# A graph network's sorting stage: bucket and target numbers read from PSUM by VectorE, totals in bank 7

## The chip, the cores and the metric

One core of one Trainium2 chip runs the whole program in one launch. The metric is the device time in microseconds (us) from the start of the execution to its end; the host only lays data out. The engines are TensorE (PE in the rows, PEld for its weight loads), VectorE (DVE), ScalarE (ACT), GpSimd (POOL) and SyncE (SP, which issues DMAs).

## The reference, cut to what matters

The graph has 6250 nodes with 128 features and 206250 edges, sorted by target node (`dst`); `src` is random. Four layers follow one another, each with a residual and a layer norm:

```python
edge_index = jnp.stack([src, dst])
x = _layernorm(x + _L0_gnn_ref(x, edge_attr_128, src, dst, ...))   # segment_sum of edge rows, 2-layer MLP
x = _layernorm(x + _L1_gnn_ref(x, edge_index, ...))                # attention over the edges
x = _layernorm(x + _L2_gnn_ref(x, edge_index, ...))                # edge MLP, segment_sum, node MLP
x = _layernorm(x + _L3_gnn_ref(x, edge_index, ...))                # normalised graph convolution
```

The change touches only the stage that computes the first layer's `segment_sum(edge_attr, receivers)` and, beside it, sorts the edges by source node for the three later layers.

## The kernel before, in words

Node features stay in SBUF, transposed, 128 features on the partitions. The edges are cut into 52 groups (`NG`) of 31 chunks (`G`) of 128 edges, 3968 edges a group, edge (p, c) of a group on partition p. The nodes fall into buckets of 128 for the sources, with one more for edges whose source is their target (`BUCKETS` is 50), and each group's targets lie in a window of 128 nodes.

The program is a row of blocks. "prepare" loads and splits the indices. Then comes "edge_sums_and_lists", the block of the change, which runs from about 107 to 812 us of the profiled execution. Each of its 52 steps does two things for one group.

The first is the sum of the edge rows by target. VectorE compares the numbers 0 to 127 with the 31 relative targets of each partition (`target_step`, L542) and so writes `dst_hot`, a float32 one-hot of 31 by 128. TensorE multiplies edge rows and one-hot, 31 products added up in PSUM bank 0 or 1 (`sum_step`, L609), and VectorE adds the result into the accumulator (`add_step`, L563). SyncE loads the edge rows, 2 MB a group, two groups ahead.

The second is the sort. VectorE compares the numbers 1 to 50 with the 31 bucket numbers of each partition (`buckets_dve`, L363) and writes `bucket_hot`, a bfloat16 one-hot of 31 by 50. TensorE counts each chunk's buckets (`totals_pe`, L369, into TOTALS in bank 2), ScalarE copies the counts to SBUF (L482), and TensorE forms running counts (`prefix_pe`, L376 and L380, in banks 3 to 6). VectorE picks each edge's own count (`pick_dve`, L387, one input in PSUM, one in SBUF), reduces it to a rank (`ranks_dve`, L401), and compares the rank with the numbers 0 to 127, each stored four times in a row (`rank_hot_dve`, L405, both inputs bfloat16 in SBUF). Meanwhile GpSimd multiplies the bucket one-hot with the edges' two values (`pay_with`, L412, two instructions a step, all operands in SBUF). TensorE multiplies rank one-hot and values (`codes_pe`, L393, into CODES in bank 7), ScalarE copies the lists (L486), TensorE transposes them (`turn_step`, L626, into TURNED in bank 7), and ScalarE copies them (L491, L495) and stores them (L497).

The order of work is written out by hand, one queue per engine, and semaphores join the queues:

- VectorE: pick and reduction of step j, bucket comparison of j+1, rank one-hot of j (it waits for the codes of j-1), target comparison of j+1, addition of j (it waits for the sum of j).
- TensorE: transposition of j-1, sum of j (it waits for the target one-hot of j), totals of j+1 (for the bucket one-hot), prefixes of j+1 (for ScalarE's copy of the totals), codes of j (for GpSimd's values, the rank one-hot and `turned_sb`).
- GpSimd: the values of j once the bucket one-hot of j is there and the codes of j-1 are done.
- ScalarE: values copied for GpSimd, the totals, the lists, the transposed lists.

`target_step` and the totals' part of TensorE's queue read so:

```python
def target_step(j, g, b):
    dve.wait_ge(summed0, j + 1)
    dve.tensor_tensor(dst_hot[b][:, :, :], over_chunks(iota, G), over_columns(of_group(rel, g), P),
                      ALU.is_equal).then_inc(hot0, 1)
...
def totals_step(j, b):
    pe.wait_ge(bucketed, j + 1)
    pe.wait_ge(totals_sb, j + 1)
    totals_pe(bucket_hot[b]).then_inc(totals_ps, 1)
```

`iota` is a 128 by 128 float32 tile in SBUF with 0 to 127 in each row, `iota1` the same plus one; `over_chunks` repeats a row for each of the 31 chunks and `over_columns` each number along a row. Re-sorts in the later stages call `buckets_dve` once each (L881 on) and use TOTALS too.

## Time and profile before

| what | value |
|---|---|
| median of 3 runs | 6396.56 us |
| lowest and highest run | 6394.72 and 6401.42 us |
| the profiled execution's own time | 6402.61 us |
| its span in the profile | 6400.8 us |
| busy over the span: TensorE, VectorE, ScalarE, GpSimd | 88%, 69%, 32%, 21% |
| mean granted TensorE clock, as a share of full speed | 0.949 |

Busy shares over the whole span mix stages with different limits, so the rows below are all of the one stage, most of it between 200 and 800 us, where every step looks like the next. In the rows, an instruction's duration runs from its start to its end as recorded; consecutive instructions of one engine overlap by some tens of ns, so the length of a chain is read from start to start. A float32 matrix product shows up as two records (62 for 31 products).

### The profile page before, as it was taken

What the parts mean: (1) busy time and instruction counts of PE and PEld (TensorE: products, weight loads), DVE (VectorE), ACT (ScalarE), POOL (GpSimd) and SP (SyncE); (2) the same over time, 40 slices, a digit from 0 to 9 for tenths busy, and PEclk for the clock granted to TensorE, in tenths of its full rate; (3) what the DMA queues carried; (4) which work ended last, traced back from release to release, by engine and by line L of the source; (5) the groups of instructions that cost most, each with busy time, mean ns of one, the idle gap of its engine ahead of it and who ended that gap; (6) DMA issues with size and microseconds to landing.
All of it is one profiled execution on the core that took longest, in us unless ns stands there. A gap on an engine that the chain in (4) does not pass through costs nothing. (4 is left out here: it accounts for less than half of the span.)

```text
span 6400.8 us, 164226 instructions
## 1 busy us (share of the span) xinstructions
PE 5654.8 (88%) x58310; PEld 4935.2 (77%) x58310; DVE 4415.6 (69%) x7547; ACT 2021.1 (32%) x4615; POOL 1361.4 (21%) x1304
## 2 busy tenths in 40 slices
PE   3999987999999999999977799989999898789987
PEld 2888876888888888888865599989899897456656
DVE  7999933777777777777764566656666564378874
ACT  0000033333333333343433222222222221366641
POOL 1444455333333333333324200000000000300000
PEclk9999999999999999999989899999999998899976
DMA  7444312222222222222211232323333221100000
GB/s 119 154 152 152 146 54 87 85 82 82 85 85 81 84 88 84 83 84 85 84 39 39 75 106 104 111 101 106 105 107 107 101 105 50 47 17 0 0 1 22
DMA packets 206497, 528.37 MB, mean 83 GB/s; under 512 B 33555, under 2 KB 85398, under 8 KB 199318
## 3 DMA queue, kind: packets, MB, share of 16 engines
q1 hardware_dynamic: 195936, 518.35, 23.8%
q8 instruction: 350, 5.73, 0.4%
q10 hardware_dynamic: 10179, 4.02, 0.3%
q14 instruction: 32, 0.26, 0.0%
HBM read 485.12 MB, written 37.19 MB: 82 GB/s over the span
## 5 line engine op out<-in xcount | busy, mean ns | idle before, releaser
L1275 PE MATMUL ps<-kv_table,stage 128*128 128x256 bf16 x7644 | 1262.6, 274 | 65.3 <-DVE stage L1131 27.3
L1247 POOL TENSOR_TENSOR message<-message 128x512 f32<-128x512 f32 (+1 forms) x676 | 725.1, 1073 | 1511.8 <-ACT message L1209 1511.8
L1663 PE MATMUL ps<-a_table,stage 128*128 128x128 bf16 x7644 | 865.7, 223 | 87.7 <-issue 56.4
L1666 PE MATMUL ps<-window,stage 128*128 128x128 bf16 x7800 | 883.5, 223 | 0.0
L1290 PE MATMUL ps<-message,slot_hot 128*128 128x136 f32 x5200 | 782.4, 293 | 112.2 <-POOL message L1247 92.9
L1565 DVE TENSOR_TENSOR slot_hot<-iota,slots 128x512 f32<-128x512 f32 (+1 forms) x676 | 454.1, 672 | 614.6 <-PE ps L1678 604.8
L1278 PE MATMUL ps<-window,stage 128*128 128x128 bf16 x7800 | 866.7, 220 | 0.0
L1290 PEld LDWEIGHTS ps<-message,slot_hot 128*128 128x128 f32 x5200 | 653.0, 191 | 201.7 <-POOL message L1247 165.6
L1138 DVE TENSOR_TENSOR slot_hot<-iota,slots 128x512 f32<-128x512 f32 (+1 forms) x676 | 452.3, 669 | 499.0 <-PE ps L1290 499.0
L1678 PE MATMUL ps<-edge,slot_hot 128*128 128x130 f32 x4992 | 731.6, 290 | 70.3 <-issue 70.3
L1616 ACT ACTIVATE edge<-ps 128x512 f32<-128x512 f32 x624 | 374.0, 599 | 1303.6 <-PE ps L1678 1266.6
L1275 PEld LDWEIGHTS ps<-kv_table,stage 128*128 128x128 bf16 x7644 | 673.1, 98 | 110.4 <-issue 55.7
L1278 PEld LDWEIGHTS ps<-window,stage 128*128 128x128 bf16 x7800 | 659.5, 99 | 62.4
L1678 PEld LDWEIGHTS ps<-edge,slot_hot 128*128 128x128 f32 x4992 | 638.9, 198 | 83.7 <-issue 83.7
L1200 ACT ACTIVATE q_kept<-ps 128x512 f32<-128x512 f32 (+1 forms) x676 | 392.7, 581 | 885.2 <-PE ps L1278 885.2
L1663 PEld LDWEIGHTS ps<-a_table,stage 128*128 128x128 bf16 x7644 | 577.0, 100 | 102.8 <-issue 92.4
L1666 PEld LDWEIGHTS ps<-window,stage 128*128 128x128 bf16 x7800 | 562.8, 100 | 0.0
L1989 PE MATMUL ps<-pairs,y_window 128*128 128x512 bf16 (+1 forms) x2028 | 532.0, 371 | 25.5 <-ACT pairs L1957 25.4
L1202 ACT ACTIVATE message<-ps 128x512 f32<-128x512 f32 (+1 forms) x676 | 392.8, 581 | 461.2 <-PE ps L1290 461.2
L1957 ACT ACTIVATE pairs<-ps 128x512 bf16<-128x512 f32 (+1 forms) x676 | 387.0, 573 | 254.6 <-PE ps L1981 207.1
L1148 DVE TENSOR_REDUCE score<-product 128x32 f32<-128x512 f32 (+1 forms) x676 | 450.0, 666 | 23.4
L1144 DVE TENSOR_TENSOR product<-ps,q_kept 128x512 f32<-128x512 f32 (+1 forms) x676 | 448.1, 663 | 5.6 <-ACT message L1202 5.6
(335 smaller groups left out, 7619.2 us busy)
## 6 DMA issues: line engine op xcount, KB each, us to landing
stage<-lists SPq DMA_DIRECT2D x312, 768.0 KB, 4.1
edges<-in_edge_attr SPq DMA_DIRECT2D x52, 1984.0 KB, 7.7
stage<-lists SPq DMA_DIRECT2D x104, 896.0 KB, 5.5
window<-qkv_rows SPq DMA_DIRECT2D x52, 288.0 KB, 4.8
qkv_rows<-kv_table SPq DMA_DIRECT2D x26, 384.0 KB, 2.5
window<-ab_rows SPq DMA_DIRECT2D x52, 192.0 KB, 4.4
qkv_rows<-q_parts SPq DMA_DIRECT2D x26, 192.0 KB, 2.0
ab_rows<-a_table SPq DMA_DIRECT2D x26, 192.0 KB, 2.0
```

The costliest lines, as they stand in the source:

```text
L1138: dve.tensor_tensor(slot_hot[n % 2][:, 0:nt, :], over_chunks(iota1[:, :], nt), over_columns(slots[:, ds(g, 1), 0, 4 * b:4 * b + nt] .rearr ...
L1144: dve.tensor_tensor(product[:, 0:nt, :], kv_ps[n % 2][:, 0:nt, 0:D], q_kept[n % 2][:, 0:nt, :], ALU.mult).then_inc(product1, 1)
L1148: dve.tensor_reduce(score[:, 0:nt, :].rearrange("p t h -> p (t h)"), product[:, 0:nt, :].rearrange("p t (h c) -> p (t h) c", c=HEAD), AX.X ...
L1247: pool.tensor_tensor(values, values, message[n % 2][:, 0:nt, D:D + HEADS].unsqueeze(3) .broadcast_to([P, nt, HEADS, HEAD]), ALU.mult).then ...
L1275: nc.tensor.matmul(kv_ps[n % 2][:, i, :], from_src, kv_table[:, tile, q, :], start=(q == 0), stop=(q == 2))
L1278: last = nc.tensor.matmul(q_ps[n % 2][:, i, :], own, window[d][:, q * D:(q + 1) * D], start=(q == 0), stop=(q == 2))
L1290: last = nc.tensor.matmul(ps[:, 6 + d, 0:D + HEADS], slot_hot[n % 2][:, i, :], message[n % 2][:, i, :], start=(tile == 0), stop=(tile == S ...
L1565: dve.tensor_tensor(slot_hot[n % 2][:, 0:nt, :], over_chunks(iota1[:, :], nt), over_columns(slots[:, ds(g, 1), 0, 4 * b:4 * b + nt] .rearr ...
L1663: nc.tensor.matmul(edge_ps[n % 2][:, i, :], from_src, a_table[:, tile, q, :], start=(q == 0), stop=False)
L1666: last = nc.tensor.matmul(edge_ps[n % 2][:, i, :], own, window[d][:, (3 + q) * D:(4 + q) * D], start=False, stop=(q == 2))
L1678: last = nc.tensor.matmul(ps[:, 6 + d, 0:D + EXTRA], slot_hot[n % 2][:, i, :], edge_of(d, b)[:, i, :], start=(tile == 0), stop=(tile == SELF))
L1989: last = nc.tensor.matmul(ps[:, 4 + quad % 2, 0:nt * P], y_window[:, ds(i * 4 + d, 1), q * D:(q + 1) * D] .rearrange("p s f -> p (s f)"), ...
```

## The change

The two rows of numbers are written once into PSUM bank 2 by TensorE (a product with the identity), on columns 128 to 383, and the two comparisons of the stage read them there. The totals, which had bank 2, go to bank 7, columns 256 on, beside CODES and TURNED; so the totals' product now also waits until ScalarE has copied the transposed lists of the step before (`turned_sb`). VectorE waits once for the numbers (`iota_set`). The re-sorts keep reading the SBUF row, and use the totals in bank 7. The one-hot of the ranks with its fours is not edited.

```diff
--- before.py
+++ after.py
@@ -351,16 +351,19 @@
         turned_sb = sem("turned_sb")
         lists_out = [sem(f"lists_out{b}") for b in range(2)]
         moved = sem("moved")
-        TOTALS = ps[0:G, 2, 0:BUCKETS]
+        iota_set = sem("iota_set")
+        IOTA_PS = ps[:, 2, P:2 * P]
+        IOTA1_PS = ps[:, 2, 2 * P:3 * P]
+        TOTALS = ps[0:G, 7, 2 * P:2 * P + BUCKETS]
         PREFIX = ps[:, 3:7, 0:8 * BUCKETS]
         CODES = ps[:, 7, 0:2 * BUCKETS]
         TURNED = ps[0:2 * TILES, 7, P:2 * P]
         GP = G + 1
         assert GP == 32 and 8 * BUCKETS <= 512 and 2 * TILES <= P
 
-        def buckets_dve(dve, hot, ids):
-
-            return dve.tensor_tensor(hot[:, 0:G, :], over_chunks(iota1[:, 0:BUCKETS], G), over_columns(ids, BUCKETS),
+        def buckets_dve(dve, hot, ids, numbers):
+
+            return dve.tensor_tensor(hot[:, 0:G, :], over_chunks(numbers[:, 0:BUCKETS], G), over_columns(ids, BUCKETS),
                                      ALU.is_equal)
 
         def totals_pe(hot):
@@ -531,15 +534,16 @@
                         dve.memset(bucket_hot[b][:, :, :], 0.0).then_inc(moved0, 1)
                         dve.memset(list_b[b][:, :, BUCKETS:TILES], 0.0).then_inc(moved0, 1)
                     dve.wait_ge(moved0, MOVE + 5)
+                    dve.wait_ge(iota_set, 1)
                     dve.sem_inc(moved, 1)
 
                     def bucket_step(j, g, b):
                         dve.wait_ge(paid, j)
-                        buckets_dve(dve, bucket_hot[b], of_group(bucket, g)).then_inc(bucketed, 1)
+                        buckets_dve(dve, bucket_hot[b], of_group(bucket, g), IOTA1_PS).then_inc(bucketed, 1)
 
                     def target_step(j, g, b):
                         dve.wait_ge(summed0, j + 1)
-                        dve.tensor_tensor(dst_hot[b][:, :, :], over_chunks(iota, G), over_columns(of_group(rel, g), P),
+                        dve.tensor_tensor(dst_hot[b][:, :, :], over_chunks(IOTA_PS, G), over_columns(of_group(rel, g), P),
                                           ALU.is_equal).then_inc(hot0, 1)
 
                     def rank_step(j, g, b, ahead):
@@ -564,7 +568,7 @@
 
                     with dve.Fori(0, total, PAIRS) as first:
                         dve.wait_ge(paid, first * 2 + 1)
-                        buckets_dve(dve, bucket_hot[0], of_group(bucket, 0)).then_inc(bucketed, 1)
+                        buckets_dve(dve, bucket_hot[0], of_group(bucket, 0), IOTA1_PS).then_inc(bucketed, 1)
                         target_step(first * 2, 0, 0)
                         rank_step(first * 2, 0, 0, True)
                         add_step(first * 2, 0, 0)
@@ -595,10 +599,13 @@
                     total = passes0(pe)
                     pe.sem_inc(prefixed, 1)
                     pe.sem_inc(coded, 1)
+                    nc.tensor.matmul(IOTA_PS, ident, iota, start=True, stop=True)
+                    nc.tensor.matmul(IOTA1_PS, ident, iota1[:, :], start=True, stop=True).then_inc(iota_set, 1)
 
                     def totals_step(j, b):
                         pe.wait_ge(bucketed, j + 1)
                         pe.wait_ge(totals_sb, j + 1)
+                        pe.wait_ge(turned_sb, j)
                         totals_pe(bucket_hot[b]).then_inc(totals_ps, 1)
 
                     def sum_step(j, pair, b):
@@ -627,6 +634,7 @@
                                          start=True, stop=True).then_inc(turned_ps, 1)
 
                     with pe.Fori(0, total, PAIRS) as first:
+                        pe.wait_ge(turned_sb, first * 2 + 1)
                         totals_step(first * 2, 0)
                         prefix_step(first * 2, 0)
                         sum_step(first * 2, first, 0)
@@ -880,7 +888,7 @@
                                          ALU.mult).then_inc(step, 1)
                 dve.tensor_scalar(r["dr1"], r["moved"], 1.0, None, ALU.add).then_inc(step, 1)
                 after(5)
-                buckets_dve(dve, r["hot"], r["bucket"]).then_inc(step, 1)
+                buckets_dve(dve, r["hot"], r["bucket"], iota1[:, :]).then_inc(step, 1)
                 after(9)
                 pick_dve(dve, r["chosen"], r["hot"]).then_inc(step, 1)
                 after(10)
```

## Rows read from the trace of the kernel before

**Rows 1.** Busy us (and instructions) of each engine, 200 to 800 us; then PEclk, DMA share, GB/s.

```profile
core 0: us, PE busy (x) PEld busy (x) DVE busy (x) ACT busy (x) POOL busy (x), PEclk, DMA share, GB/s
200.00:800.00 600.00, 545.74 (x7128) 484.73 (x7127) 593.00 (x269) 56.55 (x265) 276.07 (x90) 1.00 0.41 151
```

**Rows 2.** Groups by line, VectorE, 200 to 800 us.

```profile
line engine op names shapes xcount | busy us, mean ns | idle before us <-releasers
L542 DVE TENSOR_TENSOR dst_hot<-cst,rel 128x3968 f32<-128x3968 f32 x45 | 192.5, 4278 | 0.0
L363 DVE TENSOR_TENSOR bucket_hot<-iota,bucket 128x1550 bf16<-128x1550 f32 x45 | 143.0, 3178 | 0.0
```

**Rows 3.** Timeline, VectorE, one step: start us, duration us, instruction, idle time before.

```profile
400.14 1.81 DVE L387 TENSOR_TENSOR chosen<-ps,bucket_hot 128x1600 f32<-128x1600 f32 x1
402.10 1.82 DVE L401 TENSOR_REDUCE rank_all<-chosen 128x1600 f32 x1 [0.15 <-DVE chosen L387]
403.84 3.18 DVE L363 TENSOR_TENSOR bucket_hot<-iota,bucket 128x1550 bf16<-128x1550 f32 x1
406.94 2.28 DVE L405 TENSOR_TENSOR rank_hot<-rank_by,rank_all 128x4096 bf16<-128x4096 bf16 x1
409.14 4.28 DVE L542 TENSOR_TENSOR dst_hot<-cst,rel 128x3968 f32<-128x3968 f32 x1
413.35 0.27 DVE L563 TENSOR_TENSOR acc<-acc,ps 128x128 f32 x1
413.54 1.81 DVE L387 TENSOR_TENSOR chosen<-ps,bucket_hot 128x1600 f32<-128x1600 f32 x1
```

**Rows 4.** GpSimd's L412: two timeline entries, and its durations from 106 to 812 us.

```profile
131.94 7.04 POOL L412 TENSOR_TENSOR pay<-bucket_hot,vals 128x1550 bf16<-128x1550 bf16 x2 [10.59 <-PE ps L393]
...
399.19 6.20 POOL L412 TENSOR_TENSOR pay<-bucket_hot,vals 128x1550 bf16<-128x1550 bf16 x2 [7.20 <-PE ps L393]
...
L412 POOL TENSOR_TENSOR pay<-bucket_hot,vals x104: 2767/2954/6592, 112.0 to 804.8; 128x1550 bf16<-128x1550 bf16 x104
```

**Rows 5.** Timeline, TensorE, the same step: sum, totals, transposition, next sum.

```profile
400.07 7.19 PE L609 MATMUL ps<-dst_hot,edges 128*128 128x128 f32 x62 [0.55 <-DVE dst_hot L542]
407.19 0.97 PE L369 MATMUL ps<-bucket_hot,band 128*31 128x50 bf16 x31
...
412.65 0.26 PE L626 MATMUL ps<-ident_b,list_b 128*104 128x128 bf16 x1 [0.34 <-ACT list_b L486]
413.52 7.16 PE L609 MATMUL ps<-dst_hot,edges 128*128 128x128 f32 x62 [0.62 <-DVE dst_hot L542]
```

**Rows 6.** Timeline, TensorE: transpositions and sums, second, third and last step.

```profile
132.01 0.26 PE L626 MATMUL ps<-ident_b,list_b 128*104 128x128 bf16 x1 [0.34 <-ACT list_b L486]
132.30 7.16 PE L609 MATMUL ps<-dst_hot,edges 128*128 128x128 f32 x62
...
144.84 0.26 PE L626 MATMUL ps<-ident_b,list_b 128*104 128x128 bf16 x1 [0.34 <-ACT list_b L486]
145.43 7.16 PE L609 MATMUL ps<-dst_hot,edges 128*128 128x128 f32 x62 [0.33 <-DVE dst_hot L542]
...
802.23 7.19 PE L609 MATMUL ps<-dst_hot,edges 128*128 128x128 f32 x62 [0.56 <-DVE dst_hot L542]
```

**Rows 7.** Timeline, VectorE: block "prepare", and the first steps of the stage.

```profile
64.12 1.83 DVE L287 TENSOR_TENSOR rel<-rel,ps 128x1612 f32<-128x1612 f32 x1
...
109.19 0.06 DVE L532 MEMSET list_b<- 128x2 uint32 x1
110.01 1.77 DVE L363 TENSOR_TENSOR bucket_hot<-iota,bucket 128x1550 bf16<-128x1550 f32 x1 [0.76 <-DVE list_b L532]
111.70 4.29 DVE L542 TENSOR_TENSOR dst_hot<-cst,rel 128x3968 f32<-128x3968 f32 x1
...
136.27 4.86 DVE L405 TENSOR_TENSOR rank_hot<-rank_by,rank_all 128x4096 bf16<-128x4096 bf16 x1
```

**Rows 8.** Timeline, single instructions: ScalarE's copy, the last rank one-hot, a float32 product.

```profile
412.94 0.28 ACT L495 ACTIVATE list_i<-ps 104x128 int16<-104x128 f32 x1
...
806.00 3.70 DVE L405 TENSOR_TENSOR rank_hot<-rank_by,rank_all 128x4096 bf16<-128x4096 bf16 x1
...
819.46 0.58 PE L654 MATMUL ps<-cst,rank_max 128*1 128x128 f32 x2 [7.50 <-PEq L434]
```

## The prediction, made before the changed kernel was run

> **What bounds the kernel now.** The change touches one stage, the one named "edge_sums_and_lists", so I read that stage alone. First the table of busy time by stretch: from 200 to 800 us VectorE is busy 593.0 of 600 us, TensorE 545.7, GpSimd 276.1, ScalarE 56.6, and TensorE's granted clock is 1.00, its 2.4 GHz level [rows 1]. VectorE sets the pace, but TensorE is not far behind, and that distance caps what a faster VectorE can bring.
>
> Second, the groups by line on VectorE. The two comparisons that the change edits are L542 (targets, 3968 elements, 4278 ns) and L363 (buckets, 1550 elements, 3178 ns) [rows 2]. Per element that is 1.08 ns against 2.05 ns: the bucket comparison costs twice what its size asks for. In the stage's first step, with GpSimd not yet at work, the same line takes 1.77 us [rows 7]. So 1.41 us of each bucket comparison is not work.
>
> Third, the timelines of VectorE and GpSimd say what it is. The comparison starts at 403.84 and its result is there at 407.02 [rows 3]; GpSimd's two multiplications (L412) run from 399.19 to 405.39 [rows 4]. From 405.39 to 407.02 are 1.63 us, the 1550 elements at about 1.05 ns: it stood still until GpSimd was done, then ran. The pick (L387), whose first input is in PSUM, and the reduction (L401), with one input, lie under the same GpSimd work and take 1.81 and 1.82 us [rows 3]. Pick and target comparison differ by 2.47 us over 2368 elements, 1.04 ns each, which leaves 0.15 us fixed in either: not held. It works the other way too: the multiplications' fastest is 2767 ns, and the two together take 6.20 us instead of 5.54 [rows 4], since the first starts while the target comparison still runs.
>
> The Trainium skill (SBUF — State Buffer, section "Who interferes with whom") says that a VectorE instruction with two SBUF inputs and a GpSimd instruction that reads SBUF exclude each other for a whole instruction, and that one with at most one SBUF input does not contend. By that rule moving the numbers to PSUM ends the hold (my forecast); without it the rows leave a second reading, in which something else about the bucket comparison holds it, and the sum would be zero (the first rival). The trace agrees with the rule as far as it goes: held at L363, free at L387.
>
> **The change, part by part.**
>
> VectorE's step, from start to start: pick 1.96, reduction 1.74, bucket comparison 3.10, rank one-hot (L405) 2.20, target comparison 4.21, addition 0.19, sum 13.40 us [rows 3]. The sums on TensorE (L609) keep that pace: from 145.43 to 802.23 are 49 steps of 13.404 us [rows 6].
>
> *Bucket comparison, first input in PSUM.* Not held, it takes 1.69 us from start to start (110.01 to 111.70) [rows 7] instead of 3.10. VectorE's free step becomes 13.40 - 1.41 = 11.99 us. The price of a PSUM operand: the pick with one takes 1810 ns for 1600 elements; L287 with one, each number of it repeated, takes 1.83 us for 1612, the target comparison with both in SBUF 4.28 for 3968 [rows 3, 7]. Over 1.04 ns an element these leave 0.15, 0.15 and 0.15 us: within 0.01 us either way, and I take nothing.
>
> *Target comparison, first input in PSUM.* 4.28 us is its own length already (3968 at 1.04 and 0.15), so it stays. It only stops holding back GpSimd, whose pair shrinks from 6.20 to 5.54 us.
>
> *Rank one-hot.* It keeps two SBUF inputs. VectorE, now early, meets GpSimd with it. Reckon from the start of a sum: GpSimd starts 0.36 us before (131.94 against 132.30) [rows 4, 6] and ends at -0.36 + 5.54 = 5.18. The one-hot is held until then and needs 2.15 more (at 136.27 it shows 4.86 us and ends that much behind GpSimd's 138.98) [rows 4, 7]: 7.33. The next target comparison ends at 11.6, the addition and the pick follow, and the one-hot's next turn comes 11.99 after 5.18, at 17.17, or 4.3 into a step of 12.85: it waits 0.9 us, inside GpSimd's second multiplication. So VectorE has a hold left, in another place, and it is paid from slack: the targets are ready at 11.6, wanted at 12.85.
>
> *TensorE, the next bound.* A sum starts at 400.07 and the transposition (L626) at 412.65, 12.58 us; in between are the sum, totals, prefixes and codes without any wait for VectorE [rows 5]. What it waits for now is the target one-hot: from 412.65 to 413.52. Where the one-hot was nearly in time the sum came 0.29 us behind the transposition's start (132.01 to 132.30) [rows 6]. So its own step is 12.58 + 0.29 = 12.87; for the other parity 144.84 - 132.30 + 0.29 = 12.83. I take 12.85.
>
> *The new wait (totals for `turned_sb`).* Behind it on TensorE's queue stand totals, prefixes and codes. It asks for ScalarE's copy of the previous transposition (L495), which runs at 412.94 to 413.22 [rows 8]; the totals come 7.12 us after the sum's start (407.19) [rows 5], over 6 us later. The totals already stand behind two waits and start with no idle time. From below the price is nothing; a gain is excluded, since it removes nothing. From above it is 0.34 us, the idle time ahead of L626, where the awaited copy really comes last [rows 5], times 50 is 17 us. I take 0, the totals' own row being nearest.
>
> *Totals in bank 7.* Same 31 multiplications, same copy by ScalarE; ScalarE's other reads of that bank are 6 us away. Nothing.
>
> *Two matrix products for the numbers, and VectorE's wait for them.* Once only. TensorE has nothing to do until the first bucket comparison at 110.01 is done, and VectorE clears buffers until 109.25 and starts that comparison 0.76 us later [rows 7]. A product of this kind (float32, 128 columns) took 0.58 us [rows 8]; two are 1.2. They lie beside the clearing, which starts with the stage; with that cover gone they would cost 1.2 us once.
>
> *First and last step.* The second sum starts behind the first codes, and these behind the first sum, none of it behind VectorE [rows 6]: unchanged. At the end a held rank one-hot (806.00 to 809.70) is done 7.5 us behind the last sum's start at 802.23 [rows 6, 8]; by the reckoning above it is 7.3. Nothing.
>
> *Re-sorts in the later stages* keep their numbers in SBUF; the rest of the kernel is the same work, only sooner.
>
> **Sum.** From the second sum at 132.30 to the last at 802.23 are 669.93 us in 50 steps. At 12.85 they are 642.5. Saved: 27.4 us. VectorE's 1.41 a step would have been 71 us; 0.55 a step is what TensorE lets through. The profiled execution, 6402.6 us with a span of 6400.8, becomes 6375.2 with a span of 6373.4. It lies 6.0 us above the median of the runs, so against the 6396.6 us I say **6369 us**.
>
> **Rivals.**
>
> *The hold is not the port's* (chance 0.06). Some other trait of the bucket comparison, its bfloat16 output or second input, is slowed beside GpSimd. For it: in the steady steps it is the only slow instruction. Against: the pick has a bfloat16 second input too and is free, and the rank one-hot, where it met GpSimd, was held as well [rows 7]. VectorE stays at 13.40: 6397 us.
>
> *The hold moves instead of going* (0.04). The one-hot and GpSimd's second multiplication take turns, as at 131.94, where the pair took 7.04 us [rows 4]. Then the one-hot ends at -0.36 + 7.04 + 2.15 = 8.83, the targets at 13.1: a step of 13.1, 13 us saved, about 6384 us. Against: it needs VectorE to be there before the first multiplication is over, and a one-hot that follows the pick, which needs this step's prefixes, cannot be.
>
> *VectorE reads a broadcast row of PSUM slower while TensorE writes PSUM* (0.05), the slower side. At half rate the two comparisons' 5518 elements cost 1.04 ns more each, 5.7 us: 11.99 + 5.7 = 17.7 us a step, 4.3 more than now, over 50 steps 215 us: about 6612 us. It decides from 1.41/5518 = 0.26 ns an element upward, a quarter slower. For it: no row shows a PSUM row repeated over chunks. Against: the pick runs beside TensorE's sums at 1.04 ns.
>
> **How the numbers follow.** A measurement of this kernel can tell about 0.2%, 12.8 us. The forecast (0.85) and the rival of the moved hold just reach it. Faster 0.88, within 0.2% 0.07, slower 0.05. The low end of the range: 12.83 a step saves 28.4 us, and the runs lie 6.7 us apart: 6362. The high end: the new wait at its upper bound gives 6386, the moved hold 6384. What is left out is the first and the third rival, 0.11, and scatter.
>
> **What would show it.** Right: L363 at about 1.75 us in each step, the pick unchanged, L542 at 4.28; L412's pair at 5.5; L405 longer than 2.28, near 3.2, as the new holder of the wait; VectorE idle or held some 0.9 us a step; the sum no longer waiting for L542; sums 12.85 us apart and TensorE busy near 95% in the stage. Wrong: L363 still at 3.18 (first rival); L405 near 4.8 and L412's pair at 7 (second); L363 above 2.2 or L542 above 5.3 us with nothing on GpSimd (third); totals with idle time before them (the new wait).

## The result, and the profile after

The changed kernel took **6426.65 us** (median of 17 runs, 6404.69 to 6452.56), the kernel before 6396.56 us (17 runs on the same chip, 6383.01 to 6421.10). The ratio is 1.0042, 95% interval 1.0028 to 1.0056: slower by 0.4%, outside the 0.2% that a measurement can tell from nothing. The prediction, 6369 us (6362 to 6386) and 0.88 for faster, was wrong. The profiled execution took 6437.75 us with a span of 6435.9 us.

**The sort stage did what was predicted.** The table of busy time by stretch, changed kernel, the same columns as in [rows 1]; the last three rows are the edges of layer 1, the nodes of layer 1 and the edges of layer 2, which the prediction did not look at:

```profile
200.00:770.00 570.00, 540.91 (x7093) 481.52 (x7093) 563.16 (x267) 56.53 (x265) 244.19 (x89) 1.00 0.44 159
1047.80:3303.90 2256.10, 2083.41 (x20902) 1884.31 (x20902) 1665.85 (x3220) 869.49 (x2080) 725.42 (x676) 0.98 0.24 83
3303.90:3653.20 349.30, 241.47 (x1147) 173.18 (x1146) 157.78 (x407) 108.02 (x316) 110.84 (x208) 0.83 0.10 35
3653.20:5400.60 1747.40, 1612.54 (x20999) 1572.03 (x21000) 1091.94 (x1608) 402.65 (x727) 0.00 (x0) 0.93 0.30 105
```

In the first row TensorE is busy 540.9 of 570 us, 95%, against 91% in [rows 1]. VectorE seems as full as before (99%), but a part of that is now a held instruction. Its groups in the same stretch, and one step on its timeline (the counterparts of [rows 2] and [rows 3]; L546 is the target comparison, L366 the bucket comparison, L408 the rank one-hot, L390 the pick):

```profile
L546 DVE TENSOR_TENSOR dst_hot<-ps,rel 128x3968 f32<-128x3968 f32 x45 | 192.5, 4279 | 0.0
L408 DVE TENSOR_TENSOR rank_hot<-rank_by,rank_all 128x4096 bf16<-128x4096 bf16 x45 | 139.4, 3097 | 0.0
L366 DVE TENSOR_TENSOR bucket_hot<-ps,bucket 128x1550 bf16<-128x1550 f32 x45 | 79.3, 1762 | 0.0
```

```profile
401.85 1.82 DVE L404 TENSOR_REDUCE rank_all<-chosen 128x1600 f32 x1 [0.16 <-DVE chosen L390]
403.59 1.76 DVE L366 TENSOR_TENSOR bucket_hot<-ps,bucket 128x1550 bf16<-128x1550 f32 x1
405.27 3.21 DVE L408 TENSOR_TENSOR rank_hot<-rank_by,rank_all 128x4096 bf16<-128x4096 bf16 x1
408.40 4.28 DVE L546 TENSOR_TENSOR dst_hot<-ps,rel 128x3968 f32<-128x3968 f32 x1
```

The bucket comparison went from 3178 to 1762 ns, the target comparison stayed at 4279 against 4278 ns, and the one-hot, 2.28 us in [rows 3], is the new holder at a mean of 3.10: every step as forecast. GpSimd's pair and TensorE's step, the counterparts of [rows 4] and [rows 5]:

```profile
400.82 5.51 POOL L415 TENSOR_TENSOR pay<-bucket_hot,vals 128x1550 bf16<-128x1550 bf16 x2 [7.40 <-PE ps L396]
```

```profile
400.81 0.26 PE L633 MATMUL ps<-ident_b,list_b 128*104 128x128 bf16 x1 [0.34 <-ACT list_b L489]
401.03 7.16 PE L616 MATMUL ps<-dst_hot,edges 128*128 128x128 f32 x62
408.12 0.96 PE L372 MATMUL ps<-bucket_hot,band 128*31 128x50 bf16 x31
...
413.57 0.26 PE L633 MATMUL ps<-ident_b,list_b 128*104 128x128 bf16 x1 [0.34 <-ACT list_b L489]
413.87 0.35 PE L616 MATMUL ps<-dst_hot,edges 128*128 128x128 f32 x1
```

No idle time stands ahead of the sum (L616) any more, nor ahead of the totals (L372), behind the new wait. The second sum and the last:

```profile
132.34 7.16 PE L616 MATMUL ps<-dst_hot,edges 128*128 128x128 f32 x62
...
772.18 7.16 PE L616 MATMUL ps<-dst_hot,edges 128*128 128x128 f32 x62
```

These are 639.84 us in 50 steps, 12.80 each, against 13.40 in [rows 6]: 30.1 us saved, where 27.4 were forecast.

**The later stages gave it back, and more.** The first and last TensorE records of each stage divide both profiles (us; the sums by the start of their first and last record; the packets of code are explained below):

| kernel | sums | layer 0 begins | layer 0 | edges 1 | nodes 1 | edges 2 | nodes 2 | layer 3 | rest | packets of code: all, edges 1, edges 2 |
|---|---|---|---|---|---|---|---|---|---|---|
| before | 117.1 to 809.1 | 827.9 | 250.5 | 2224.6 | 332.9 | 1727.7 | 254.6 | 593.8 | 177.5 | 350, 101, 227 |
| changed | 117.0 to 779.1 | 797.8 | 250.0 | 2256.1 | 349.3 | 1747.9 | 254.7 | 593.7 | 177.2 | 476, 227, 227 |

The changed kernel enters layer 0 30.1 us sooner. Then it loses 31.5 us in the edges of layer 1, 16.4 in its nodes and 20.2 in the edges of layer 2, in code that the change does not touch. In which instructions, the groups on TensorE say (busy us, mean ns of one, idle time before them). The kernel before, edges of layer 1 (1078.4 to 3303 us), then of layer 2 (3635.9 to 5363.2):

```profile
L1275 PE MATMUL ps<-kv_table,stage 128*128 128x256 bf16 x7644 | 1262.6, 274 | 65.3 <-DVE stage L1131 27.3 <-issue 26.7 <-DVE product L1144 11.3
...
L1290 PE MATMUL ps<-message,slot_hot 128*128 128x136 f32 x5200 | 782.4, 293 | 112.2 <-POOL message L1247 92.9
...
L1666 PE MATMUL ps<-window,stage 128*128 128x128 bf16 x7800 | 883.5, 223 | 0.0
L1663 PE MATMUL ps<-a_table,stage 128*128 128x128 bf16 x7644 | 865.7, 223 | 87.7 <-issue 56.4 <-DVE stage L1546 31.3
L1678 PE MATMUL ps<-edge,slot_hot 128*128 128x130 f32 x4992 | 731.6, 290 | 70.3 <-issue 70.3
```

The changed kernel, the same two stages:

```profile
L1283 PE MATMUL ps<-kv_table,stage 128*128 128x256 bf16 x7644 | 1266.8, 275 | 97.8 <-DVE product L1152 60.8 <-DVE stage L1139 27.0 <-issue 10.0
...
L1298 PE MATMUL ps<-message,slot_hot 128*128 128x136 f32 x5200 | 786.2, 294 | 101.9 <-POOL message L1255 82.8
...
L1674 PE MATMUL ps<-window,stage 128*128 128x128 bf16 x7800 | 896.0, 225 | 78.1 <-issue 78.1
L1671 PE MATMUL ps<-a_table,stage 128*128 128x128 bf16 x7644 | 872.6, 225 | 88.0 <-issue 56.7 <-DVE stage L1554 31.3
L1686 PE MATMUL ps<-edge,slot_hot 128*128 128x130 f32 x4991 | 724.7, 289 | 0.0
```

In the edges of layer 1 TensorE stands idle 32.5 us longer ahead of one line, L1275, now L1283. Some 10 us of that come back ahead of L1298, which waits less for GpSimd than L1290 did, and 9.1 us are added because the same products take longer (busy 2083.41 against 2074.31 us): together nearly all of the 31.5. The timeline of L1283 there, changed kernel, only the entries with over 1.5 us of idle time before them, from the stage's start on:

```profile
1047.81 0.80 PE L1283 MATMUL ps<-kv_table,stage 128*128 128x256 bf16 x3 [27.00 <-DVE stage L1139]
1224.95 0.80 PE L1283 MATMUL ps<-kv_table,stage 128*128 128x256 bf16 x3 [2.92 <-DVE product L1152]
1312.01 0.49 PE L1283 MATMUL ps<-kv_table,stage 128*128 128x256 bf16 x3 [2.79 <-DVE product L1152]
1397.71 0.49 PE L1283 MATMUL ps<-kv_table,stage 128*128 128x256 bf16 x3 [2.98 <-DVE product L1152]
1485.42 0.80 PE L1283 MATMUL ps<-kv_table,stage 128*128 128x256 bf16 x3 [3.34 <-issue]
```

From 1224.95 on they are about 87 us apart, one for each turn of the stage's loop, and stand where the loop begins again. The cause that the row names is not to be trusted. VectorE's "product" (L1152) started at 1396.32 and took 0.68 us, so it was over at 1397.00, and the three records behind this idle time start at 1397.71; in other turns the same idle time is put down to "issue", that is, to nothing that the profile shows. In the kernel before such idle times stand at the head of some turns only: none between 1343 and 1516 us, where a turn began at about 1430. In the edges of layer 2 both kernels have two of them in every turn, which takes about 68 us: one at the loop's head (L1663, L1671), and one some 5 us later, once the code has run on a little. One turn of the kernel before, then one of the changed kernel:

```profile
3760.32 0.34 PE L1663 MATMUL ps<-a_table,stage 128*128 128x128 bf16 x3 [2.27 <-issue]
3765.75 1.46 PE L1678 MATMUL ps<-edge,slot_hot 128*128 128x130 f32 x6 [2.44 <-issue]
```

```profile
3777.83 0.43 PE L1671 MATMUL ps<-a_table,stage 128*128 128x128 bf16 x3 [2.49 <-issue]
3782.83 0.29 PE L1674 MATMUL ps<-window,stage 128*128 128x128 bf16 x1 [2.43 <-issue]
```

Counted from the loop's head, the second stands ahead of the 27th product before (24 gathering products, two of the eight at L1678, then the stop) and ahead of the 24th in the changed kernel: the same code stands still at another instruction.

What came with it is in the list of the DMA queues (packets, MB, share of 16 engines' time). The whole of the kernel before, and the whole of the changed one:

```profile
q8 instruction: 350, 5.73, 0.4%
```

```profile
q8 instruction: 476, 7.80, 0.5%
```

This queue brings code, in packets of 5.73 MB / 350 = 16.4 kB, taken here as 256 instructions of 64 bytes. Experiment 2 tests a shift by 256, and in experiments 3 to 6 the program of some 16,000 instructions on TensorE comes in 63 packets, about 256 to each. The change adds 126 packets, and the same list by stage puts all of them into the edges of layer 1: 101 before, 227 after. A stage without repeated fetching has 20 (see below), and 227 - 20 = 207 = 23 times 9: all 23 jumps back of the loop's 24 turns bring 9 packets. In the kernel before they were 101 - 20 = 81, 9 turns. The packets and the idle times go together turn by turn: in the kernel before, nine packets of code start between 1339 and 1414 us, around a turn that begins with idle time (at 1343), and none between 1416 and 1510 us, in the turn that begins without it.

**The theory** from this, ahead of the experiments: the two matrix products and the wait make TensorE's compiled program 9 instructions longer (8 of them the products, since a float32 product is two passes of a weight load and a multiplication) and shift all its later loops by 9 places. The other engines' programs have their old length. TensorE keeps its code in blocks of 256 instructions. The loop of layer 1's edges has 1702 instructions. Within 7 blocks it stays where it is; reaching into an eighth, it is fetched anew. Its head stands at place 100 of a block before and 109 after (places counted from 0), so that its last instruction has place 9 of an eighth block before, and 18 after (where the blocks begin was worked out from the places of the idle times, and is part of what is tested). The rivals: the kernel's later stages are slower by the 30 us by which they start sooner, or by a clock level that came by chance, or by PSUM's bank 2 or 7.

### The profile page after: what moved, and what is told of

The parts are those of the page before. It is cut to its first block and busy times, and to the rows that moved or that the text cites. A ratio compares the mean times of both kernels' runs of the same rounds, so it can differ in the third digit from the quotient of the medians.

```text
span 6435.9 us, 164235 instructions
## 1 busy us (share of the span) xinstructions
PE 5689.5 (88%) x58314; PEld 4961.9 (77%) x58314; DVE 4386.3 (68%) x7547; ACT 2021.6 (31%) x4615; POOL 1323.2 (21%) x1304
## 5 line engine op out<-in xcount | busy, mean ns | idle before, releaser
L1283 PE MATMUL ps<-kv_table,stage 128*128 128x256 bf16 x7644 | 1266.8, 275 | 97.8 <-DVE product L1152 60.8
L1674 PE MATMUL ps<-window,stage 128*128 128x128 bf16 x7800 | 896.0, 225 | 78.1 <-issue 78.1
L1671 PE MATMUL ps<-a_table,stage 128*128 128x128 bf16 x7644 | 872.6, 225 | 88.0 <-issue 56.7
L1298 PE MATMUL ps<-message,slot_hot 128*128 128x136 f32 x5200 | 786.2, 294 | 101.9 <-POOL message L1255 82.8
L1298 PEld LDWEIGHTS ps<-message,slot_hot 128*128 128x128 f32 x5200 | 657.0, 192 | 189.0 <-POOL message L1255 165.3
L1283 PEld LDWEIGHTS ps<-kv_table,stage 128*128 128x128 bf16 x7644 | 674.3, 99 | 146.0 <-DVE product L1152 71.6
L1671 PEld LDWEIGHTS ps<-a_table,stage 128*128 128x128 bf16 x7644 | 581.6, 101 | 103.0 <-issue 92.7
L1152 DVE TENSOR_TENSOR product<-ps,q_kept 128x512 f32<-128x512 f32 (+1 forms) x676 | 448.8, 664 | 5.7 <-ACT message L1210 5.7
```

The source lines that it names most:

```text
L1152: dve.tensor_tensor(product[:, 0:nt, :], kv_ps[n % 2][:, 0:nt, 0:D], q_kept[n % 2][:, 0:nt, :], ALU.mult).then_inc(product1, 1)
L1283: nc.tensor.matmul(kv_ps[n % 2][:, i, :], from_src, kv_table[:, tile, q, :], start=(q == 0), stop=(q == 2))
L1298: last = nc.tensor.matmul(ps[:, 6 + d, 0:D + HEADS], slot_hot[n % 2][:, i, :], message[n % 2][:, i, :], start=(tile == 0), stop=(tile == S ...
L1671: nc.tensor.matmul(edge_ps[n % 2][:, i, :], from_src, a_table[:, tile, q, :], start=(q == 0), stop=False)
L1674: last = nc.tensor.matmul(edge_ps[n % 2][:, i, :], own, window[d][:, (3 + q) * D:(4 + q) * D], start=False, stop=(q == 2))
```

## The experiments

Ten kernels, in three series, each with runs of the kernel before on the same chip (its medians: 6399.76, 6385.91 and 6401.00 us). Most add the same edit, fillers: increments of a semaphore that nobody waits for, in the block "prepare", ahead of all loops on TensorE. They do nothing but shift the code that follows.

```diff
                     last.then_inc(low_ready, 1)
+                    for _ in range(9):
+                        pe.sem_inc(pe_waited, 1)
```

**1. The kernel before, 9 fillers** (the shift without the change).

> The kernel before, with nothing but nine semaphore increments more on TensorE's queue, in the block "prepare", where TensorE waits for loads from 55 to 107 us. The changed kernel's TensorE program is nine instructions longer than before. Theory, placement: what costs the time is that the loops of the later stages lie nine instructions further on, so that the loop of layer1_edges (1702 instructions) has its code loaded anew on every turn: instruction queue 476 packets as after, against 350 before; layer1_edges about 2256 us against 2225; the kernel about 6440 us against 6397, slower although nothing of the sort is changed. Rival, the later stages suffer from the change's own edits (totals in bank 7, numbers in bank 2, another phase of the clock because the sort ends 30 us sooner): this kernel has none of them, 350 packets and 6397 us.

Measured: 6457.92 us (6446.75 to 6472.74), ratio 1.0103 [1.0064, 1.0141], 476 packets, 227 of them in the edges of layer 1, which took 2264.4 us. The slowdown comes without any of the change's parts, without an earlier start (layer 0 begins at 828.8) and without a new use of PSUM. The edges of layer 2 took 1747.9 us, exactly as in the changed kernel; the nodes of layer 1 took 336.8, near the 332.9 of the kernel before and not the 349.3 of the changed one. With the 31 us of experiment 4 taken off, 0.5%, this ratio would be 1.0055, within the interval of the change's own.

**2. The changed kernel, 247 fillers** (256 - 9, so that every loop has the place in its blocks that it had in the kernel before).

> The changed kernel with 247 semaphore increments at the same idle place, so that 9 + 247 = 256 instructions lie ahead of the later loops: by placement that is where they were before, if code is loaded in blocks of 256 instructions. Placement: about 350 packets plus one, give or take some turns (before, only some turns of layer1_edges loaded their code), layer1_edges near 2225 us, the sort's 30 us kept: about 6369 us. Rival, the change's own edits: 476 packets or so, later stages as after, about 6427 us.

Measured: 6367.34 us (6336.56 to 6388.06, 10 runs), ratio 0.9951 [0.9930, 0.9971], 324 packets, 74 in the edges of layer 1 (6 turns), 2203.7 us there. With the loops placed as in the kernel before, the change is 32 us faster (19 to 45 by the interval), where 27 were predicted. That the time lies 2 us from the predicted 6369 is partly luck: in its profile 6 turns fetched and not 9, which made the edges of layer 1 20.9 us shorter than in the kernel before. The edges of layer 2 took 1729.6 us (1727.7 before), and their second idle time is back ahead of the third of the eight products, as it must be if 256 places are a whole number of blocks:

```profile
3719.03 0.83 PE L1688 MATMUL ps<-edge,slot_hot 128*128 128x130 f32 x6 [1.61 <-issue]
```

**3 and 4. Both kernels, placed so that both loops fit within 7 blocks** (149 fillers in the changed kernel, 158 in the kernel before, which brings both to the same places).

> The changed kernel with 149 increments. By placement (loads of 256 instructions, eight kept at a time, the block boundary 64 instructions off as the stall at the window products of layer2_edges shows it: before the 27th matrix product after the loop's head in the changed kernel, before the 30th in the kernel before) both loops, 1702 and 1685 instructions, now lie in seven blocks each, and neither is loaded anew: about 350 - 91 - 217 = 40 packets; layer1_edges about 2190 us, layer2_edges about 1580 us (its 46 stalls of 2.2 to 4.0 us gone), the kernel about 6210 us. Rival: no effect, 6427 us; a partial one, if only one of the loops is freed: 227 packets fewer and 6370 us or 6250 us.

> The kernel before with 158 increments: the later loops stand where they stand in the changed kernel with 149. Placement: about 40 packets, layer1_edges and layer2_edges as long as in that kernel to within 5 us, and the kernel 27 to 30 us longer than it, about 6240 us: the change's own worth with placement held equal is -30 us. Rival, the change costs the later stages something of its own: this kernel would be faster than the changed one with 149.

Measured: 6136.15 us (6127.94 to 6142.63), ratio 0.9596 [0.9563, 0.9628], and 6167.17 us (6156.73 to 6180.07), ratio 0.9648 [0.9614, 0.9681]; 63 packets each. The times lie well under the expected 6210 and 6240 us, and 40 packets were expected: the direction was right, the size of what fetching costs was not. (The two products that the expectation names, the 27th and the 30th, are the 24th and the 27th in the traces.) The change is worth 6167.17 - 6136.15 = 31.0 us where the placement is the same. And the placement alone is worth 3.5% to the kernel before, far more than the change: 49.6 us in the edges of layer 1 and 198.3 in those of layer 2. Two other stages differ too, but in opposite directions and not by the placement: the nodes of layer 1 are 21.0 us longer, the "rest" is 19.8 shorter. Stage by stage:

| kernel | sums | layer 0 begins | layer 0 | edges 1 | nodes 1 | edges 2 | nodes 2 | layer 3 | rest | packets of code |
|---|---|---|---|---|---|---|---|---|---|---|
| changed, 149 | 118.4 to 780.6 | 799.4 | 250.6 | 2176.9 | 352.9 | 1529.4 | 254.7 | 593.3 | 157.7 | 63, 20, 19 |
| before, 158 | 117.9 to 809.4 | 828.4 | 251.2 | 2175.0 | 353.9 | 1529.4 | 254.7 | 593.4 | 157.7 | 63, 20, 19 |

The groups of experiment 3 on TensorE, first those of the edges of layer 1, then of layer 2:

```profile
L1285 PE MATMUL ps<-kv_table,stage 128*128 128x256 bf16 x7644 | 1252.9, 273 | 28.4 <-DVE stage L1141 27.6 <-DVE product L1154 0.8
...
L1676 PE MATMUL ps<-window,stage 128*128 128x128 bf16 x7800 | 861.3, 219 | 0.0
L1673 PE MATMUL ps<-a_table,stage 128*128 128x128 bf16 x7644 | 843.6, 219 | 31.3 <-DVE stage L1556 31.3
L1688 PE MATMUL ps<-edge,slot_hot 128*128 128x130 f32 x4985 | 696.3, 282 | 0.0
```

The 60.8 us put down to VectorE's product are 0.8, and every "issue" entry is gone; the one wait left is the stage's entry, the first turn's wait for the first gather one-hot. The table by stretch shows the edges of layer 2:

```profile
3579.50:5108.00 1528.50, 1528.25 (x20993) 1501.31 (x20994) 1091.31 (x1608) 402.22 (x726) 0.00 (x0) 1.00 0.34 117
```

TensorE is busy 1528.25 of 1528.50 us at a granted clock of 1.00, its 2.4 GHz level, where the changed kernel had 1612.54 of 1747.40 at 0.93. A fetch costs more than its idle time: of the 218 us between the two, 134.6 are idle time and 84.3 the same work done slower. The clock falls behind the idle times. The changed kernel ahead of a turn's two idle times (3775.3 to 3777.8 and 3780.4 to 3782.8), right behind them, and later in the turn:

```profile
3765.00:3775.00 10.00, 10.00 (x144) 9.94 (x142) 6.86 (x11) 2.79 (x5) 0.00 (x0) 1.00 0.21 80
3783.00:3787.00 4.00, 4.00 (x29) 3.91 (x29) 0.69 (x1) 0.60 (x1) 0.00 (x0) 0.50 0.01 4
3800.00:3840.00 40.00, 40.00 (x553) 39.41 (x550) 28.78 (x42) 10.52 (x19) 0.00 (x0) 1.00 0.37 127
```

The column behind the engines is the granted clock: 1.00, then 0.50 (its 1.2 GHz level), then 1.00 again.

**5. The bucket comparison's edit alone** (the target comparison reads SBUF again; products, waits and 149 fillers stay).

```diff
-    dve.tensor_tensor(dst_hot[b][:, :, :], over_chunks(IOTA_PS, G), ...
+    dve.tensor_tensor(dst_hot[b][:, :, :], over_chunks(iota, G), ...
```

> The changed kernel with 149 filler instructions (as the run before of that placement), whose target comparison reads its numbers from SBUF again, so that it costs about 0.05 us more or less; the bucket comparison keeps its numbers in PSUM. TensorE's code has the same length and place, so the code traffic should be the 63 packets of that run and the later stages its 1529 us in the edges of layer 2. Theory (the sort stage is bound by TensorE's 12.8 us per step once the bucket comparison is no longer held by GpSimd): sort stage within 1 us of the fully changed kernel (sums from 118.4 to 780.6), whole kernel within 10 us of 6136. Rival (the target comparison, 4.3 us long, takes a real part of the gain): steps of 12.9 us or more, the stage over 5 us longer, the whole at 6141 or more.

Measured: 6122.91 us (6111.77 to 6131.63), ratio 0.9597 [0.9562, 0.9631]. From the second sum to the start of the last record: 128.88 to 775.6, 646.7 us, as in experiment 3 (133.86 to 780.6, 646.7). The edit of the target comparison adds nothing to that of the bucket comparison; the rival is out. (The whole time is 13 us under the expected 6136; the kernel before was 14 us faster on this chip too, and the ratio is that of experiment 3.) The two groups, L368 the bucket and L548 the target comparison:

```profile
L548 DVE TENSOR_TENSOR dst_hot<-cst,rel 128x3968 f32<-128x3968 f32 x45 | 192.5, 4278 | 0.0
...
L368 DVE TENSOR_TENSOR bucket_hot<-ps,bucket 128x1550 bf16<-128x1550 f32 x44 | 77.5, 1762 | 0.0
```

**6. The target comparison's edit alone** (the bucket comparison reads `iota1` in SBUF again, at both calls).

```diff
-    buckets_dve(dve, bucket_hot[b], of_group(bucket, g), IOTA1_PS).then_inc(bucketed, 1)
+    buckets_dve(dve, bucket_hot[b], of_group(bucket, g), iota1[:, :]).then_inc(bucketed, 1)
```

> The changed kernel with 149 filler instructions, whose bucket comparison alone reads its numbers from SBUF again. Theory: it is held again until GpSimd's pair has ended, but the pair is shorter since the target comparison no longer slows it (5.5 instead of 6.2 us), so the chain of the step is worked out as 13.05 us against 13.40 before and 12.8 with both edits: the stage is some 12 us longer than with both, the whole near 6149. Rival A (the hold costs what it did before, the shorter pair brings nothing): steps of 13.4 us, the stage 30 us longer, the whole near 6167. Rival B (the hold was harmless): steps of 12.8 us, 6136.

Measured: 6132.36 us (6118.77 to 6150.33), ratio 0.9603 [0.9570, 0.9637], which the whole time does not set apart from experiment 5 (6149 us were expected, on the scale of the first series). The stage does: the sums run from 129.09 to 783.39, 50 steps of 13.09 us (13.05 expected, 13.40 and 12.80 the rivals). VectorE's groups, and its bucket comparisons and GpSimd's pairs in two steps:

```profile
L368 DVE TENSOR_TENSOR bucket_hot<-iota,bucket 128x1550 bf16<-128x1550 f32 x44 | 125.7, 2857 | 0.0
```

```profile
407.24 3.27 DVE L368 TENSOR_TENSOR bucket_hot<-iota,bucket 128x1550 bf16<-128x1550 f32 x1
...
420.73 2.46 DVE L368 TENSOR_TENSOR bucket_hot<-iota,bucket 128x1550 bf16<-128x1550 f32 x1
```

```profile
403.37 5.51 POOL L417 TENSOR_TENSOR pay<-bucket_hot,vals 128x1550 bf16<-128x1550 bf16 x2 [7.98 <-PE ps L398]
416.05 5.51 POOL L417 TENSOR_TENSOR pay<-bucket_hot,vals 128x1550 bf16<-128x1550 bf16 x2 [7.17 <-PE ps L398]
```

The pair is at 5.51 us although the bucket comparison waits on it. The second pair starts at 416.05 while the target comparison still runs (to 416.91), as in the kernel before, and is no longer slowed: it was the target comparison with two SBUF inputs that made the pair 6.20 us, as the prediction said. In experiment 5 it has two SBUF inputs again, and the pair still takes 5.51 us, because VectorE is early and the target comparison is over before the pair starts (409.22 against 410.04). The first comparison ends at 410.51, 1.63 us after its pair (408.88), the second at 423.19, 1.63 us after its pair (421.56): held again until GpSimd's end. The mean of the steps was right, but they are not even: the sums are 13.39 us apart here and 12.8 in the next step.

**7. The kernel before, 4 fillers** (the loop of layer 1 ends at place 13 of its eighth block).

> The kernel before with 4 filler instructions on TensorE ahead of all loops, nothing else changed. In the kernel before, the loop of the edges of layer 1 ends on the 9th instruction of its last block of 256 and its code was fetched anew on 9 of its turns; with 9 fillers it ends 9 instructions later and is fetched anew on every turn. Theory (a race between the fetch that runs ahead and the jump back, decided by how far into the last block the loop reaches): a number of turns between those two, so 350 to 476 packets of code, the edges of layer 1 at 2225 to 2256 us, the edges of layer 2 unchanged at 227 packets. Rival (another border passed between 0 and 9, or something that has nothing to do with the place): exactly 350 or 476 packets, by a jump.

Measured: 6395.28 us (6365.82 to 6412.91, 10 runs), ratio 1.0007 [0.9985, 1.0029]; 332 packets, 83 in the edges of layer 1 (7 turns), 2213.1 us there. Fewer than at place 9, not more, which fits neither side: the count did not grow with the distance, and two profiles with the loop at place 9 already differ by more (9 turns before, 6 in experiment 2).

**8. The kernel before, 246 fillers** (ten places back: the loop of layer 1 ends with the last instruction of its seventh block, that of layer 2 still reaches into an eighth).

> The kernel before with 246 fillers on TensorE ahead of all loops, so that by the block model the loop of the edges of layer 1 fits within 7 blocks of 256 instructions and ends with the last instruction of the seventh, while the loop of the edges of layer 2 still reaches into an eighth. Theory: the loop of layer 1 is fetched once (about 20 packets, 2176 us as in the runs without reloads), the loop of layer 2 is still fetched on every turn (227 packets, 1728 to 1748 us), about 270 packets in all, and the whole about 40 to 50 us under the kernel before. Rival (the fillers or the total length of the code matter, not where each loop lies): both loops change alike, either both near 20 packets (6167 us) or both above 200 (6450 us).

Measured: 6299.98 us (6290.45 to 6309.75), ratio 0.9869 [0.9834, 0.9905]; 270 packets, 19 and 227. The edges of layer 1 took 2176.2 us, as expected to the microsecond; those of layer 2 1691.1, under the 1728 to 1748 expected. The two loops are set apart by where each lies: the rival, fillers as such, is out. The whole is 86 us under the kernel before, where 40 to 50 were expected, in part because the fetches of layer 2 cost less here though as many packets came. Its second idle time stands at the same line (L1680 here is L1678 of the kernel before) but ahead of the last of the eight products, not the third: five products of two instructions, so the ten places. It is shorter in sum:

```profile
L1665 PE MATMUL ps<-a_table,stage 128*128 128x128 bf16 x7644 | 860.2, 222 | 84.7 <-issue 54.2 <-DVE stage L1548 30.5
L1680 PE MATMUL ps<-edge,slot_hot 128*128 128x130 f32 x4992 | 721.4, 287 | 52.0 <-issue 52.0
```

```profile
3726.59 0.27 PE L1680 MATMUL ps<-edge,slot_hot 128*128 128x130 f32 x1 [3.06 <-issue]
```

So with the same 227 packets the second idle time summed to 70.3 us in the kernel before, 78.1 in the changed one and 52.0 here.

**9. The change with one product instead of two** (the buckets' numbers 1 to 50 are columns 1 to 50 of the first product; real code in place of fillers).

```diff
-        IOTA1_PS = ps[:, 2, 2 * P:3 * P]
+        IOTA1_PS = ps[:, 2, P + 1:P + 1 + BUCKETS]
...
-                    nc.tensor.matmul(IOTA_PS, ident, iota, start=True, stop=True)
-                    nc.tensor.matmul(IOTA1_PS, ident, iota1[:, :], start=True, stop=True).then_inc(iota_set, 1)
+                    nc.tensor.matmul(IOTA_PS, ident, iota, start=True, stop=True).then_inc(iota_set, 1)
```

> The changed kernel with no filler, but with one product for the numbers instead of two: the buckets' numbers 1 to 50 are columns 1 to 50 of the first product's result. TensorE's code is 4 instructions shorter than the changed kernel's and 5 longer than that of the kernel before, so the loop of layer 1's edges reaches 14 instructions into its last block (9 in the kernel before, 13 with 4 fillers, 18 in the changed kernel). Theory (where the loops lie is all that the change lost by): the code of that loop is fetched anew on some turns only, 83 to 130 packets in it and 330 to 380 in all, the edges of layer 1 between 2205 and 2230 us, the sort stage as changed (sums to 779), and the whole near 6367, the time that was predicted for the change. Rival (14 is already too far into the block): 227 packets, 476 in all, 2256 us, the whole at 6425.

Measured: 6439.08 us (6422.74 to 6450.21, 6 runs), ratio 1.0057 [1.0035, 1.0079]; 476 packets, 227 in the edges of layer 1, 2264.4 us there. The rival was right: with its end at place 14, the loop is fetched on every turn. The forecast of a time near 6367 us for this kernel was wrong by 72 us.

**10. The kernel before, 7 fillers** (its end at place 16).

> The kernel before with 7 fillers, the loop of layer 1's edges ending 16 instructions into its last block. Theory (a race, more often lost the further the loop reaches in): between the 83 packets at 13 and the 227 at 18 in that loop, so some 90 to 200, 340 to 450 in all. Rival (a hard border between 13 and 18): exactly 227, 476 in all, or no more than the 83 to 101 seen at 13 and 9.

Measured: 6461.60 us (6443.71 to 6483.66), ratio 1.0079 [1.0049, 1.0109]; 476 packets, 227 in the edges of layer 1, 2266.3 us. The rival again. Together, by where in its eighth block the loop of layer 1's edges ends (one profile for each entry):

| place of the last instruction in the eighth block | packets there | turns with a fetch, of 23 | edges 1, us |
|---|---|---|---|
| none (experiments 3 to 6, 8) | 19 to 20 | 0 | 2175 to 2177 |
| 9 (before; changed with 247) | 101; 74 | 9; 6 | 2224.6; 2203.7 |
| 13 (before with 4) | 83 | 7 | 2213.1 |
| 14 (one product) | 227 | 23 | 2264.4 |
| 16 (before with 7) | 227 | 23 | 2266.3 |
| 18 (changed; before with 9) | 227 | 23 | 2256.1; 2264.4 |

My picture of a race that is lost the more often the further the loop reaches in is wrong. In these profiles there are three cases: never, on 6 to 9 of 23 turns, and from 14 on always. Why only some turns fetch at 9 and 13, and whether 14 is a border elsewhere, was not tried. The places are counted from one origin, worked out from one idle time, so the counts could be off by a few instructions alike; their differences are exact.

## Why the prediction was wrong

It failed in one sentence: "*Re-sorts in the later stages* keep their numbers in SBUF; the rest of the kernel is the same work, only sooner." And, ahead of it, in the step "*Two matrix products for the numbers, and VectorE's wait for them.* Once only", which costed their execution (1.2 us, hidden, rightly) and not their place in TensorE's program. The same work was not the same code to the chip: 9 instructions further on, the loop of layer 1's edges was fetched on 23 turns instead of 9 (31.5 us in the profile; 9 is that profile's number, the same placement gave 6 in experiment 2), and the fetch in layer 2's loop fell at another instruction (20.2 us, of them 7.8 more idle time, the rest mostly the same work at a clock of 0.93 instead of 0.94). That the shift does it and nothing else of the change is shown by experiment 1 (shift without change: slower) and by 2, 3 and 4 (change without shift: faster, by 31 us in 3 and 4). Layer 2's part moved with the placement too: 1747.9 us in experiment 1, 1729.6 in experiment 2. The third loss, 16.4 us in the nodes of layer 1, is not the placement's: that stage took 333 to 354 us in all these profiles without regard to the places (352.9 and 353.9 us in experiments 3 and 4, 336.2 in experiment 5 with the same places, 336.8 in experiment 1 with those of the changed kernel). It goes by the granted clock, 0.90 and 0.83 in the two profiles; what sets it was not tried. So the change costs -30 + 31 + 20 = 21 us by the profiles, and 30 by the medians, whose interval, 18 to 36 us, holds it.

The rest of the working, by its steps:

- *Bucket comparison*, 1.69 us from start to start unheld: 1.68 (403.59 to 405.27). The rule of the Trainium skill on which the forecast leaned (SBUF — State Buffer, "Who interferes with whom") held, both ways: experiment 5 moves one operand and frees the instruction, experiment 6 moves it back and it is held until GpSimd's end. The rival "the hold is not the port's" is out.
- *Target comparison*, 4.28 us unchanged, and GpSimd's pair from 6.20 to 5.54: 4279 ns and 5.51 us. "VectorE reads a broadcast row of PSUM slower" is out. As a whole this part of the edit was not needed: without it (experiment 5) the stage takes the same time.
- *Rank one-hot*, to wait 0.9 us for GpSimd's second multiplication: 3.10 against 2.28, 0.82 us. It is in the chain of VectorE but is paid from slack. "The hold moves instead of going" is out: 12.80, not 13.1.
- *TensorE, the next bound*, 12.85 us: 12.80, the one term with a gap, 2.5 us over the stage. From a sum's start to the transposition were 12.54 us (12.58 taken), and from there to the next sum 0.22 and 0.30 (0.29 taken for both parities); so TensorE's step was right to 0.05 us and the stage's 30.1 us against 27.4 is no luck.
- *The new wait* and *totals in bank 7*, nothing: no idle time ahead of L372.

The sum's sign turned on something that none of the rivals held. The slower side had 0.05, all of it on PSUM reads in the stage itself. The queue of code (350 packets for a program whose TensorE part has some 16,000 instructions, 63 blocks) stood in the profile of before, with 227 of the packets in one loop, and the "issue" idle time in that loop was 56.4 + 70.3 us. Whoever had read these rows could not have told where the border lies, but could have put a chance on a loop that sits near one.

The Trainium skill does have a warning (Runtime: NRT & Kernel Launch, "Instruction fetch mechanics"): code comes in blocks of 256 instructions, TensorE's store holds 2048, and a jump back whose target is outside the current window of two blocks makes the engine wait. The packets of 16.4 kB, 63 for some 16,000 instructions, agree with the blocks of 256. The window of two does not hold here: loops over 7 blocks ran 24 turns with 19 to 20 packets in the stage (experiments 3 to 6). A store of 2048 would be 8 blocks, and loops that reach into an eighth were fetched anew; that one of the eight is taken up by the block fetched ahead would fit the ninth packet of each such turn, but no run shows it. The section also calls the cost of crossing a block "mostly hidden". Here a turn with a fetch costs (2256.1 - 2176.9) / 23 = 3.4 us in layer 1 and (1747.9 - 1529.4) / 23 = 9.5 us in layer 2; by the same sum the 9 turns of the kernel before cost (2224.6 - 2176.9) / 9 = 5.3 us each in layer 1, so that the price of a turn isn't a constant.

**A version that beats both** is the changed kernel with 149 fillers, or its bucket edit alone with them: 6136 and 6123 us, ratios 0.9596 and 0.9597, 4% below the kernel before. Of these 4% the placement brings 3.5 and the change 0.5.

## What to carry to other kernels

A change that adds instructions ahead of a long loop on an engine also moves that loop in the engine's code store, and a loop of nearly 7 blocks of 256 instructions can pay for 9 instructions with more than the change brings. Look at the count of code packets in the list of DMA queues before and after, by stage: if it differs, compare the two kernels at the same placement, with fillers, before judging the edit. Idle time at a loop's head, once a turn, put down to "issue" or to an instruction that was over before the idle time was, is the mark of it, and idle instructions that bring the loop within 7 blocks (149 and 158 here) can be worth more than the tuning.

## What the runs showed that was not expected

- The code of a loop of 1702 instructions was fetched never, on 6 to 9 of 23 turns, or always, as it ended within its seventh block, or at place 9 to 13, or 14 to 18, of an eighth; a turn that fetches brings 9 packets, the whole loop and one more, not the one block that is missing.
- The fetch costs twice: it stops the engine, and the clock is lower behind it. In the edges of layer 2 the 1747.9 us of the changed kernel held 134.6 us of idle time beyond experiment 3's and 84.3 us of the same multiplications at a lower granted clock (0.93 against 1.00 over the stage, 0.50 right behind the idle times).
- The same number of packets costs differently by where the border between two blocks cuts the loop: the edges of layer 2 took 1727.7, 1747.9 and 1691.1 us (before, changed, experiment 8) with 227 packets each. What makes a cut cheap was not tried.
- Two stages that the change doesn't touch take one time or another in profiles of the same placement: the nodes of layer 1 333 to 354 us, at a granted clock from 0.90 down to 0.82, and the last stretch (the "rest") 158 to 178 us, at 0.80 down to 0.63. What sets the clock there was not tried; each is as large as a part of the effect studied here, so a comparison stage by stage is worth more than one of the whole.
